# An attention and mixture-of-experts kernel: GpSimd's low weight parts at other places of its queue, and a batch's first maximum and norm statistics in front of its router columns

## What is computed

```python
x = L0_attn_x                                   # 4 batches of 1024 tokens, 128 numbers each
h = layernorm(x)
scores = einsum('nsd,ntd->nst', h * w_lhs, h * w_rhs)
x = x + einsum('nst,ntd->nsd', softmax(scores, axis=2), h)
h2 = layernorm(x)
probs = softmax(h2 @ router_w.T)                # 8 experts, the best two of each token are used
combine = the two largest probs of a token, divided by their sum
hid = gelu_tanh(einsum('nc,ech->neh', h2, w_fc) + b_fc)        # 512 hidden numbers per expert
out = einsum('neh,ehc->nec', hid, w_proj) + b_proj
return x + einsum('nec,ne->nc', out, combine)
```

## Time and profile before

| what | value |
|---|---|
| median of 3 runs | 331.57 us (331.29 to 331.64) |
| profiled execution | 331.83 us, span 330.1 us |
| TensorE matmuls busy | 280.7 us (85%) |
| TensorE weight loads busy | 250.0 us (76%) |
| VectorE busy | 225.1 us (68%) |
| ScalarE busy | 192.6 us (58%) |
| GpSimd busy | 185.5 us (56%) |
| mean granted TensorE clock | 0.948 |

### The profile page before, as it was taken

The page is one execution under the profiler, slowest core; times in us unless marked ns, Lnnn a source line. Parts: engine busy times, 40 slices in busy tenths (PEclk is TensorE's granted clock), DMA queues, the critical chain, the costliest instruction groups (busy, mean ns, idle before and its releaser), DMA issues.

```text
span 330.1 us, 7870 instructions
## 1 busy us (share of the span) xinstructions
PE 280.7 (85%) x2197; PEld 250.0 (76%) x2198; DVE 225.1 (68%) x894; ACT 192.6 (58%) x388; POOL 185.5 (56%) x247
## 2 busy tenths in 40 slices
PE   8999998989979995995979999899999999994000
PEld 3588995878858894784968999799999999993000
DVE  4898879898867789799689778345444545453065
ACT  3455567957195634754389877567676767670000
POOL 8030035380777526768778777777777755567200
PEclk9999999999999999799899999999999999998555
DMA  6940000030011100101511531343333321111398
GB/s 204 426 203 0 0 3 0 3 118 13 18 42 43 34 14 29 50 26 42 156 45 44 131 109 52 93 135 101 99 91 88 91 81 47 50 42 48 116 354 317
DMA packets 16948, 29.37 MB, mean 89 GB/s; under 512 B 3760, under 2 KB 12848, under 8 KB 16656
## 3 DMA queue, kind: packets, MB, share of 16 engines
q1 hardware_dynamic: 12080, 18.40, 17.5%
q0 software_dynamic: 4832, 10.53, 9.6%
HBM read 16.30 MB, written 12.62 MB: 88 GB/s over the span
## 4 chain that ended last, share of the span: by engine, by line
PE 59%; DVE 21%; DMA 6%; issue 5%; POOL 4%; ACT 2%; SPq 1%; POOLq 0%; DVEq 0%; ACTq 0%
PE av_ps L1302 17%; PE av_ps L1099 14%; DVE neg_piece L1409 6%; PE sc_ps L1281 4%; PE sc_ps L1282 4%; PE sc_ps L1283 4%; DMA raw_proj<-results 4%; PE bank L1269 2%; PE bank L1088 2%; PE sc_ps L1088 1%; PE bank L1075 1%; DVE tile_start L534 1%; PE bank L1077 1%; PE bank L1076 1%; PE sc_ps L1076 1%
## 5 line engine op out<-in xcount | busy, mean ns | idle before, releaser
L873 POOL DMA_INDIRECT results<-prob,result_row x78 | 74.8, 959 | 32.0 <-issue 12.8
L774 POOL DMA_INDIRECT slots<-stage,slot x64 | 63.6, 993 | 39.1 <-DVE stage L1569 18.8
L1099 PE MATMUL av_ps<-h_all,prob 128*128 128x137 f32 x512 | 73.9, 289 | 3.6 <-DVE lg_part L1440 3.6
L1016 ACT ACTIVATE raw_fc<-sc_ps,bfc,scale_down 128x256 f32<-128x256 f32 x156 | 75.1, 570 | 2.1 <-PE sc_ps L1283 2.1
L1302 PE MATMUL av_ps<-raw_proj,raw_fc 128*128 x624 | 75.8, 275 | 0.0
L1099 PEld LDWEIGHTS av_ps<-h_all,prob 128*128 128x128 f32 x512 | 68.1, 194 | 7.4 <-DVE res L1437 5.1
L1302 PEld LDWEIGHTS av_ps<-raw_proj,raw_fc 128*128 128x128 f32 x624 | 72.6, 192 | 0.5
L1746 DVE TENSOR_TENSOR h_all<-av_ps,bpr 128x256 f32<-128x256 f32 x39 | 16.5, 424 | 48.9 <-PE sc_ps L1283 46.5
L1281 PE MATMUL sc_ps<-h_all,wfc_hi 128*128 128x256 f16 x156 | 42.6, 273 | 1.3 <-ACT raw_fc L1016 1.1
L1008 ACT ACTIVATE h_all<-bank 128x512 f16<-128x512 f16 x39 | 23.2, 596 | 34.5 <-PE sc_ps L1283 30.7
L1282 PE MATMUL sc_ps<-h_all,wfc_hi 128*128 128x256 f16 x156 | 42.5, 273 | 0.0
(11 more groups left out here) (183 smaller groups left out, 508.4 us busy)
## 6 DMA issues: line engine op xcount, KB each, us to landing
slots_in<-slots SPq DMA_DIRECT2D x39, 132.0 KB, 2.2
raw_fc<-in_w_fc_dram SPq DMA_DIRECT2D x1, 2048.0 KB, 10.9
raw_proj<-in_w_proj_dram SPq DMA_DIRECT2D x1, 2048.0 KB, 15.2
raw_fc<-results SPq DMA_DIRECT2D x2, 1024.0 KB, 7.4
raw_proj<-results SPq DMA_DIRECT2D x2, 1024.0 KB, 12.0
out_dram<-res SPq DMA_DIRECT2D x4, 512.0 KB, 5.0
res<-in_x_dram SPq DMA_DIRECT2D x3, 512.0 KB, 5.8
results<-prob,result_row POOLq DMA_INDIRECT x78, 2.3
```

Of the source, the lines that this page charges most:

```text
L774: pool.indirect_dma_start(out=slots[:, :], out_offset=bass.IndirectOffsetOnAxis(ap=slot[:, n, k:k + 1], axis=0), in_=stage[:, b % 2, t, :] ...
L873: pool.indirect_dma_start(out=results[:, :], out_offset=bass.IndirectOffsetOnAxis(ap=result_row[a][:, h:h + 1], axis=0), in_=gated[a][h], ...
L1016: ins = act.activation(hid[:, a % NH, c, :], up_ps(a, c), ACT.Gelu_apprx_tanh, bias=bfc[:, e, c:c + 1], scale=scale_down[:, 0:1])
L1099: mm = pe.matmul(att[:, t, 0:AUG], probT[:, m % RING, t * P:(t + 1) * P], h_aug[:, b % 2, exp_rows(n), :], start=(n % BT == 0 and t % 2 == ...
```

## The change

On GpSimd: parts 0 and 1 move to the end of batch 0's round, in front of `scale_ln2(0)`. Part 2 stays at the head of batch 1. Parts 3 and 4 with the padding move behind `gate_powers` and behind a new wait for the reciprocal of `add_attention(2)`. Parts 5 to 7 move behind the first scatter of batch 2 and a new wait for the reciprocal of `add_attention(6)`. On VectorE: `row_max(b + 1, 0)`, `add_logits(2b)` and `take_stats2(2b)` move in front of `keep_hrw(b + 1)`. Four steps of the first table move from the end of batch 2 into batch 3. In batch 3 all four `shift_again` come in front of `find_slots`.

```diff
+            def beside_sums(u):
+
+                pool.wait_ge(inv_made, u + 1)
+
...
             for b in range(B):
                 if b == 1:
-                    for i in range(3):
-                        low_part(i)
+                    low_part(2)
                 if b == 2:
                     dispatch_max(b - 2)
                     dispatch_next(b - 2, 0)
...
                 if b >= 1:
                     scale_ln2(2 * b - 1)
+                if b >= 2:
+                    dispatch_next(b - 2, 1)
+                if b >= 1:
+                    gate_powers(ROUNDS_BY[b - 1] - 1)
                 if b == 1:
+                    beside_sums(2 * b)
                     for i in range(3, EMPTY_PIECES):
                         low_part(i)
                     clear_empty()
                     for half in range(2):
                         store_empty(half)
-                if b >= 2:
-                    dispatch_next(b - 2, 1)
-                if b >= 1:
-                    gate_powers(ROUNDS_BY[b - 1] - 1)
                 if b == B - 1:
+                    dispatch(B - 2, 0)
+                    beside_sums(2 * b)
                     for i in range(EMPTY_PIECES, PIECES):
                         low_part(i)
...
                 if b + 2 < B:
                     scale(2 * b + 4)
                     scale(2 * b + 5)
+                if b == 0:
+                    low_part(0)
+                    low_part(1)
                 if b + 1 < B:
                     scale_ln2(2 * b)
...
-            for i in range(5):
+            for i in range(1, 5):
                 dispatch(B - 2, i)
             scale_ln2(2 * B - 2)
...
                 for n in range(8):
-                    row_max(b, n)
-                    if b >= 1 and n == 0:
-                        add_logits(2 * b - 2)
-                        take_stats2(2 * b - 2)
+                    if b == 0 or n >= 1:
+                        row_max(b, n)
...
                 if b == B - 1:
-                    steps(first_table, 7)
+                    steps(first_table, 10)
...
                 add_attention(2 * b)
-                for r in (0, 1):
+                for r in range(TU) if b == B - 1 else (0, 1):
                     shift_again(b, r)
...
-                for r in (2, 3):
-                    shift_again(b, r)
+                if b + 1 < B:
+                    for r in (2, 3):
+                        shift_again(b, r)
...
                 if b + 1 < B:
+
+                    row_max(b + 1, 0)
+                    add_logits(2 * b)
+                    take_stats2(2 * b)
                     keep_hrw(b + 1)
-                if b == B - 2:
-                    steps(first_table, 4)
```

## The result

The changed kernel takes 330.07 us in the median of 20 runs (327.32 to 334.74), the kernel before 331.65 (331.04 to 334.42), 1.6 us less. The ratio of the two is 0.9908, with an interval of 0.9887 to 0.9929, or 3.05 us less (2.4 to 3.7), and it is taken over fast runs alone: it leaves out nine of the changed kernel's 20, which took 332.51 to 334.74 at a mean clock of 0.93 to 0.94, where the other eleven took 327.32 to 330.13 at 0.94 to 0.96. The forecast was 3.4 us less, 328.2; the profiled execution took 328.69, its span is 326.9 where it was 330.1.

The account below looks back on a forecast made before the run. No engine was taken to bound the whole kernel; each stage was read by itself, with GpSimd's queue counting from batch 3's sums. 0.8 + 0.86 − 0.3 + 1.9 + 0.15 = 3.4 us off 331.57 gave 328.2, range 326.8 to 330.6.

Parts of the forecast that it names:

- rival 3: Batch 3's head gives nothing, as score 8 or GpSimd's scale holds the turn, or half clock lasts longer: 330.1; chance 0.12.
- What the stalls are: GpSimd's two-input SBUF reads hold four VectorE instructions until the last back-to-back part; moved, those lines return to their medians.
- rival 1: PSUM-and-SBUF inputs wait for GpSimd too, so parts 3 and 4 hold batch 1's sums by 2.3 us: 332.6; chance 0.09.
- Batch 1's two stalls: Moving parts 0, 1, 3 and 4 brings TensorE 0.8 us at the maxima and 0.86 at the shift, sum 1.66.
- the new neighbours: Batch 1's head: x_logits product and variance beside parts 0 and 1 may wait up to 1.13 us each, covered by the gain.
- The late stores: Batch 1's DRAM stores move behind part 4, holding the first scatter 0 to 0.3 us; 0.3 taken, with the split's loss.
- far end of 1.2: The most that the first scatter would be held, in us, if the two moved stores are slow.
- Head of batch 3: Filling VectorE's 0.89 us wait and moving four table steps of about 0.25 out gains 1.9 us, arriving in full.
- the low end's vanished stretch: A half-clock stretch at 132 may vanish, which puts the range's low end 0.2 us below the forecast's own.
- Parts 5 to 7: Before batch 3's second sums: TensorE's 3.62 us idle shrinks, but GpSimd's queue then counts; net gain 0.15, from −0.5 to 0.5.
- the wait for the moments: GpSimd's one wait for VectorE among its scatters, 0.45 us at 161.26, counted as helping cover a 1.6 us clock loss.
- Rival 2: The gain from batch 3's stall arrives as well, GpSimd's queue not being the bound: 323.3; chance 0.06.

Follow-up runs that it names:

- e1: Changed kernel with GpSimd's parts 5 to 7 back right behind batch 3's gates' power, first scatter behind them, no reciprocal wait: median 334.22 us, ratio 0.9949.
- e3: Changed kernel with VectorE's order at the heads of batches 1 to 3 and the four table steps put back: median 332.43 us, ratio 1.0021.
- e2: Changed kernel with parts 3 and 4, the padding and its two stores back in front of batch 1's gates' power: median 328.82 us, ratio 0.9919.
- e4: Changed kernel with batch 3's two norm scales on GpSimd moved in front of the first table's scatters in batch 1: median 326.45 us, ratio 0.9847.
- e9: Changed kernel with two extra unread powers on GpSimd ahead of the 15 scatters of batch 2: median 335.98 us, ratio 1.0113.
- e10: Changed kernel with parts 5 to 7 a batch earlier and batch 3's norm scales in front of the first table's scatters: median 323.9 us, ratio 0.9769.
- e5: Changed kernel with two extra unread GpSimd powers, on a slower chip: 364.83 us against 368.37 for the kernel before, ratio 0.9877.
- e7: Changed kernel with parts 5 to 7 made a batch earlier, on a slower chip: 364.7 us against 368.37 for the kernel before, ratio 0.9886.
- e11: Changed kernel with 16 unread matmuls before tile 8's wait, on a slower chip: 362.64 us against 364.45 for the kernel before, ratio 0.9947.
- e6: Changed kernel with 16 unread matmuls before tile 8's wait, on a slower chip: 362.2 us against 368.37 for the kernel before, ratio 0.9812.
- e8: Changed kernel with parts 5 to 7 a batch earlier and batch 3's norm scales forward, slower chip: 363.04 us against 368.37 for the kernel before, ratio 0.982.
- e12: e10's kernel with the last table's scatters moved forward, on a slower chip: 363.81 us against 364.45 for the kernel before, ratio 0.9989.

## Why the prediction was right

By the ratio 3.05 us came off, and 3.4 had been forecast. The median of all runs, 330.07, lies in the range, 0.5 us below its upper end, at the number of rival 3 (330.1); what tells the two apart is the ledger.

**What the stalls are, and that they go:** right. All four lines are at their medians, the routing step behind parts 5 to 7 took 0.88, where I had written up to 1 us, and e1 brings 4.00 us back on whichever two-input step is next. By the Trainium skill (SBUF — State Buffer, Who interferes with whom) an instruction of VectorE with at most one SBUF input, outside its two-port modes, does not contend with GpSimd. The trace agrees: the form with one PSUM and one SBUF tensor, on which rival 1 hung, runs beside the parts at 0.34 and 0.68 us as elsewhere. Rival 1 is out.

One reading was too simple: that a stalled step waits until the last back-to-back part is over. It does for the three parts at 150.76 (4.01 us), whose records leave no gap. But parts 3 and 4 of the kernel before leave 0.09 us between them:

```profile
64.79 1.17 POOL L748 TENSOR_TENSOR wfc_lo<-raw_fc,wfc_hi 128x512 f16<-128x512 f32 x1
...
66.05 1.17 POOL L748 TENSOR_TENSOR wfc_lo<-raw_fc,wfc_hi 128x512 f16<-128x512 f32 x1
```

L1514 got through in that gap, after 1.16 us, and L1518 was held by the second part. The router product beside parts 0 and 1 got through between them too, after 0.63 us. It changed no term of the sum.

**Batch 1's two stalls, 1.66:** right in kind, too small. The turn came 0.95 earlier (0.8 predicted), the reciprocal 2.06. A whole idle of 0.86 was counted as the most that TensorE could take at the second stall; by the ledger it took 1.11. And e3 shows that the 0.95 hangs on VectorE's order at the head, which I said gives nothing: without it 1.24 would be lost beside parts 0 and 1. I had written that the new neighbours might wait up to one part and that the gain covers that; it does (the product waits 0.41), but by the order, not of itself.

**The late stores, −0.3: this is the term that was mis-sized.** By the ledger 2.06 at the reciprocal is 0.61 at the first scatter and 0.62 at batch 2's turn: 1.4 lost. I had them issued at 78.5 and 0.9 later on the old clock of events; with batch 1 2.06 ahead that is 76.4 and 77.3, and they went out at 76.32 and 77.4, right to 0.1. The scatter's other condition, the metadata, ran 2.02 ahead as well, so it is right too. What failed is one step, the landing: I took the 4.0 of the page for both stores, which is the middle between 3.7 and 4.4, and in their new place it was 3.7 and 5.0:

```profile
DMA to landing us min/median/max: 3.7/4.4/5.0
```

That is 1.0 more for the later of the two, which holds the scatter, and it makes 1.4 of my 0.3. My far end of 1.2, "if the stores are slow", should have been the value, and was still a little short. Batch 1 returned 0.62, and e2, which undoes this part, measures no difference. It is no chance of one execution: 3.7 and 5.0 (once 5.1) stand in ten profiles that have the stores at the new place, 5.1 and 6.0 in the two with the added powers, and 3.7 and 4.4 in the two that have them at the old one. Nor is it the amount moved, as the DMA engines are busy for 3.1 us in both places, with next to nothing else. Why they land later there is open.

**Head of batch 3, 1.9:** 1.99 between the metadata and the second maximum (2.62 less the 0.63 at the metadata), all of it at the turn at 129.24 (2.59), 1.98 by e3. Rival 3 is out. The idle of 2.17 stayed as it was, as it is ScalarE's chain behind the last maximum, and the granted clock behind it is 1.00 where before it was 0.50: the low end's vanished stretch, some 0.3 us more at the gate (146.85 against 149.73, 2.88). That part is luck: the same idle of 2.15 to 2.17 us stands there in e1, e2, e3, e4 and e9, and the clock fell behind it in all of them but e4.

**Parts 5 to 7, 0.15:** right that TensorE's gain would be lost again: it reached the experts 7.75 us earlier (157.08 against 164.83), and then stood 3.86 in front of tile 8 (some 4 predicted), with a clock of 0.57 behind it. The net on GpSimd's queue was 0.45, the wait for the moments that I had named; at tile 16 the gain is 2.43 only, 0.8 less than at tile 8. Here a step failed: the 1.6 us of half clock behind tile 8 were to be nearly covered by the wait of 1.29 at tile 16. TensorE's own time between the two turns, waits taken off, grew by 1.7 (26.87 to 28.57), and the wait gave back 0.86. The traces show that the last scatter has ceased to be the bound there: the turn of tile 16 comes 5.44, 5.47 and 5.51 us behind its start in the kernel before, in e10 and in e1, where TensorE waits over 1.2 us for it, but 6.54 in the changed kernel, 6.55 in e2, 6.10 in e3, 6.98 in e4 and 7.08 in e9, which all had half clock behind tile 8. Measured by that bound, the half clock costs 1.1 us at tile 16 in the changed kernel and 0.6 to 1.6 in the others. The whole part was a loss of 0.4, within the bounds of 0.5 that I gave. e9 and e10 show the bound at tile 8 from both sides: work put on GpSimd's queue came through in full (3.19), and the 1.11 by which scatter 15 moved came through as 1.18. Rival 2, with 323.3, is out; e10 shows what it takes to get there.

**The sum.** 3.4 was predicted, 3.05 measured (2.4 to 3.7). Term by term, from the two profiles:

| term | predicted | measured |
|---|---|---|
| batch 1's two stalls | 1.66 | 2.06 |
| late stores | −0.3 | −1.44 |
| head of batch 3 | 1.9 | 1.99 |
| clock behind its turn | 0 | 0.3 |
| parts 5 to 7, with the clock behind tile 8 | 0.15 | 0.45 − 0.84 |
| sum at tile 16 | 3.4 | 2.5 (ledger 2.43) |

At the end the last result goes back 2.61 us earlier (304.13 against 306.74), and the span is 3.2 shorter because the last load from the results took 12.22 us and not 12.86. So the sum is close by luck in part: the stores and parts 5 to 7 came out 1.1 and 0.5 us worse than forecast, batch 1, the clock at 132 and that last load 0.4, 0.3 and 0.6 better, and the last was in nobody's sum.

## What to carry to other kernels

Where one engine's two-input reads hold another's, look for long back-to-back runs of them and move them beside work that takes one operand from PSUM; where the run has no gap, the cost of meeting it is not one instruction but the whole run (three parts, 4.0 us). But follow everything that is queued behind the moved run: here two stores went with it, and the gain of the stage ended at their landing, which small, independent work put in front of the wait would hide (e4, 2 us). An engine that leads gains nothing from a stall removed while another one's queue feeds it: shorten that queue (e10).

## What I had not expected

**An idle in front of a turn can cost its time again in clock, in one run and not in the next.** Up to batch 2's turn the changed kernel and e1 are the same program, with 2.95 and 2.96 us of idle in front of it. In the changed kernel's profile the clock behind it is 1.00, in e1's (length, busy times, clock) it is not:

```profile
92.00:98.00 6.00, 5.48 (x14) 3.69 (x13) 2.54 (x8) 4.33 (x10) 4.67 (x5) 0.51 0.17 56
```

and batch 2's second turn is 2.6 later (110.25 against 107.64). In e9 the first scatter waits 6.10, TensorE idles 3.87, and 0.57 follows for 8 us. Of all 14 profiles, eight have 2.79 to 3.87 us of idle there, and the clock fell behind it in six (e1, e3, e5, e7, e9, e11) and not in two (the changed kernel and e6, both 2.95); six have 0.67 to 1.55 (the kernel before, e2, e4, e8, e10, e12), and it fell in none by 100 us. So the moved stores made an idle at 92 on which the clock can fall. e2's runs lie within 2.5 us of each other and e4's within 3.2, the changed kernel's within 7.4 and e1's within 9.7; but e3's 12 runs lie within 2.6, with an idle of 2.79. That this idle is what parts the changed kernel's runs into the eleven up to 330.13 and the nine from 332.51 on is what these rows suggest, not something that a run isolates. If it is, the nine are a price of the change, and its gain is nearer to the 1.6 us of the medians than to the 3.05 of the ratio; e4, which takes the idle away, is 3.6 us below the changed kernel by the medians.

**The same program differs by 10% from chip to chip:** 331.7, 364.5 and 368.4 us for the kernel before. In the kernels profiled on the slower two TensorE has 12 to 20 us of gaps in issue. I do not know what holds its instructions there.
